# Attention weights stored as (query, four heads), with key tiles added in pairs for the denominator

## The reference

```python
q = (x @ Wq + bq).reshape(n, H, DK); k = ...; v = ...
logits = einsum('ehd,ehd->eh', q[rows] * scale, k[cols]) + att_bias
row_max = segment_max(logits, rows)
p = exp(logits - row_max[rows])
denom = segment_sum(p, rows)
att = p / denom[rows]
y = segment_sum(att[:, :, None] * v[cols], rows)
out = y.reshape(n, H * DK) @ Wo + bo
x = layernorm(x + out)
```

## Time and profile before

| | before |
|---|---|
| median of 3 runs (lowest to highest) | 1270.24 us (1258.51 to 1271.98) |
| profiled execution: span of the core | 1264.5 us |
| mean granted TensorE clock | 0.987 |
| PE busy | 1203.6 us (95%) |
| DVE busy | 864.5 us (68%) |
| ACT busy | 431.7 us (34%) |
| attention loop, first scores to last denominator product | about 982.6 to 1250.4 us of the span |

### The profile page before, as it was taken

The page is one execution under the profiler, slowest core; times in us unless marked ns, Lnnn a source line. Parts: engine busy times, 40 slices in busy tenths (PEclk is TensorE's granted clock), DMA queues, the critical chain, the costliest instruction groups (busy, mean ns, idle before and its releaser), DMA issues.

```text
span 1264.5 us, 22058 instructions
## 1 busy us (share of the span) xinstructions
PE 1203.6 (95%) x8483; PEld 547.2 (43%) x8484; DVE 864.5 (68%) x1180; ACT 431.7 (34%) x585; POOL 309.5 (24%) x220
## 2 busy tenths in 40 slices
PE   6989888999898999999999999999999999999997
PEld 2334333323443343344445454454332455555563
DVE  7577666434444555552478874658999799899897
ACT  1445556322232221213301003145551454444344
POOL 2001110000010243454555654555462000000000
PEclk9989999999998999999999999999999899999999
DMA  8568885798798788643122213113222666465552
GB/s 325 208 225 301 292 298 165 281 358 310 244 360 284 276 313 278 220 97 114 3 50 35 50 3 69 2 2 44 33 33 56 234 206 230 167 203 198 189 181 107
DMA packets 64414, 222.78 MB, mean 176 GB/s; under 512 B 31226, under 2 KB 36090, under 8 KB 48360
## 3 DMA queue, kind: packets, MB, share of 16 engines
q1 hardware_dynamic: 34794, 156.40, 35.6%
q0 software_dynamic: 25184, 53.10, 16.5%
q10 hardware_dynamic: 4350, 12.07, 2.8%
HBM read 198.94 MB, written 59.94 MB: 205 GB/s over the span
## 4 chain that ended last, share of the span: by engine, by line
PE 64%; DVE 11%; DMA 10%; issue 8%; SPq 5%; ACT 3%; ACTq 0%; DVEq 0%
PE PS L1812 24%; PE PS L1761 10%; PE PS L2057 4%; PE PS L1616 4%; PE PS L2044 4%; DMA R<-R 4%; DVE R L1147 4%; DVE R L1182 3%; PE PS L1634 3%; SPq L602 3%; PE PS L1686 2%; PE PS L1926 2%; SPq L600 2%; PE PS L2077 2%; PE PS L2106 2%
## 5 line engine op out<-in xcount | busy, mean ns | idle before, releaser
L787 POOL DMA_INDIRECT bias_d<-R x160 | 272.9, 1706 | 331.5 <-DMA bias_d<-R 220.2
L1812 PE MATMUL PS<-R 128*128 128x512 f16 x1300 | 298.4, 381 | 0.0
L1812 PEld LDWEIGHTS PS<-R 128*128 128x128 f16 x1300 | 120.5, 98 | 180.5 <-issue 49.8
L1572 ACT ACTIVATE R<-PS 128x1024 f32<-128x1024 f32 (+1 forms) x100 | 100.4, 1005 | 144.0 <-PE PS L2044 143.9
L1686 PE MATMUL PS<-R,XX 125*128 125x512 f16 (+2 forms) x612 | 131.0, 344 | 16.2 <-ACT R L1361 7.5
L1761 PE MATMUL PS<-W,XX 128*128 128x512 f16 x600 | 136.1, 386 | 4.7 <-DVE R L985 2.7
L1182 DVE SCALAR_TENSOR_TENSOR R<-R,W 128x1024 f32<-128x1024 f32 (+1 forms) x68 | 133.9, 1985 | 8.7 <-ACT R L1572 7.2
L1147 DVE CUSTOM_DVE_ANT_0 R<-PS,R 128x1250 f16<-128x1250 f32 x80 | 116.8, 1460 | 5.5 <-PE PS L1980 2.9
L901 DVE TENSOR_SCALAR R<-W,R 125x1250 f16<-125x1250 f16 x160 | 89.5, 606 | 42.4 <-PE PS L1686 27.6
L2044 PE MATMUL PS<-R 128*128 128x256 f16 (+3 forms) x800 | 107.4, 277 | 1.4 <-DVE R L1147 1.1
L2057 PE MATMUL PS<-R 128*32 128x256 f32 (+1 forms) x1600 | 105.7, 382 | 0.7 <-DVE R L1182 0.3
(11 more groups left out here) (226 smaller groups left out, 1395.6 us busy)
## 6 DMA issues: line engine op xcount, KB each, us to landing
bias_d<-bias_d POOLq DMA_DIRECT2D x39, 1280.0 KB, 8.5
R<-in_basis_s SPq DMA_DIRECT2D x32, 1024.0 KB, 6.6
W<-in_basis_s SPq DMA_DIRECT2D x28, 1024.0 KB, 6.3
W<-bias_d SPq DMA_DIRECT2D x27, 1024.0 KB, 4.9
R<-bias_d SPq DMA_DIRECT2D x13, 1024.0 KB, 5.0
R<-key_d SPq DMA_DIRECT2D x20, 500.0 KB, 3.8
R<-R SPq DMA_DIRECT2D x120, 80.0 KB, 5.9
W<-bias_d SPq DMA_DIRECT2D x7, 904.0 KB, 4.6
```

The source lines that it names most:

```text
L787: pool.indirect_dma_start(bias_d, bass.IndirectOffsetOnAxis(ap=idx[:, c:c + 1], axis=0), attr[:, c, :], None, bounds_check=DUMP + GC * P - ...
L1572: S.activation(ER[:, n % 4, :].rearrange("p (h r) -> p h r", h=4)[:, :, 0:w], PS[:, 2 * (n % 2):2 * (n % 2) + 2, :].rearrange("p a (e r) - ...
L1812: ins = T.matmul(mm_out(SUM_BANK(s, i), D), lhs, rhs, start=n == 0, stop=n == len(terms) - 1)
```

## The change

The weights now lie as (query, four heads) in `ER`. ACT writes each head's 256 values 16 bytes apart, DVE reads bias in runs of four neighbouring heads and weights in one run, and PE reads each head's columns in 16-byte steps. DVE adds the weights of two consecutive key tiles of the same head group into a buffer `SR` (two of them), and PE makes the denominator products from that sum once per two tiles. `ORDER` starts and ends with two key tiles in place of three for each group. The third bias buffer, the buffers `SR` and the f16 copy of Wo (`Wo16`) get other places in SBUF, so that SP's wait for the row maxima ahead of the third bias load is no longer needed and is left out.

```diff
--- before.py
+++ after.py
@@ -235,7 +235,8 @@
         bdf = tmp2(2 * EC).rearrange("p (g e) -> p g e", g=2)
         btf = tmp2(CH)
 
-        o = 2 * HEADS * NN // 2 + NN // 2 + RB
+        KEPT = 2 * HEADS * NN // 2 + NN // 2 + RB
+        o = KEPT
 
         def kept(n):
             nonlocal o
@@ -295,13 +296,20 @@
         o3 = NT * D + FT * RB
         y16 = XX[:, o3:o3 + FT * RB].bitcast(F16).rearrange("p (q f n) -> p q f n", q=2, f=FT)
         o3 += FT * RB
-        Wo16 = XX[:, o3:o3 + FT * D].bitcast(F16).rearrange("p (q f n) -> p q f n", q=2, f=FT)
-        assert o3 + FT * D <= NT * D + FT * NN
+        def quad_major(region):
+
+            return region.rearrange("p (r h) -> p r h", h=4)
+
         BW = 4 * RB
-        BR = [w_b[:, 0:2 * BW], w_b[:, 2 * BW:4 * BW], r1f[:, half:half + 2 * BW]]
-        ER = r1f[:, half + 2 * BW:half + 6 * BW].rearrange("p (s n) -> p s n", s=4)
-        assert 6 * BW <= half
+        BR = [w_b[:, 0:2 * BW], w_b[:, 2 * BW:4 * BW], XX[:, o3:o3 + 2 * BW]]
         NB = len(BR)
+        o3 += 2 * BW
+        SR = [quad_major(r) for r in (XX[:, o3:o3 + BW], r2[:, KEPT:KEPT + BW])]
+        assert o3 + BW <= NT * D + FT * NN and KEPT + BW <= NT * NN
+        Wo16 = r1f[:, half:half + FT * D].bitcast(F16).rearrange("p (q f n) -> p q f n", q=2, f=FT)
+        o4 = half + FT * D
+        ER = [quad_major(r1f[:, o4 + s * BW:o4 + (s + 1) * BW]) for s in range(4)]
+        assert FT * D + 4 * BW <= half
         Wo = W[:, 2, :, :]
 
         PS = ctx.enter_context(nc.psum_tensor("PS", [P, 8, 512], F32))
@@ -422,6 +430,7 @@
         st_done = sem("st_done")
         e_made = sem("e_made")
         p_made = sem("p_made")
+        sum_made = sem("sum_made")
         pv_done = sem("pv_done")
         den_read = sem("den_read")
         den_first_read = sem("den_first_read")
@@ -533,10 +542,17 @@
             return b16[32 * (n % 4):32 * (n % 4) + 2, n // 4, :], ones16[32 * (n % 4):32 * (n % 4) + 2, :]
 
 
-        ORDER = [(t, q) for q in range(QUADS) for t in range(NB)]
-        ORDER += [(t, q) for t in range(NB, NRB * NT - NB) for q in range(QUADS)]
-        ORDER += [(t, q) for q in range(QUADS) for t in range(NRB * NT - NB, NRB * NT)]
-        LATE = [n for n in range(STEPS - NB, STEPS)]
+        ORDER = [(t, q) for q in range(QUADS) for t in range(2)]
+        ORDER += [(t, q) for t in range(2, NRB * NT - 2) for q in range(QUADS)]
+        ORDER += [(t, q) for q in range(QUADS) for t in range(NRB * NT - 2, NRB * NT)]
+        PAIRS = [(ORDER.index((t - 1, q)), n) for n, (t, q) in enumerate(ORDER) if t % 2]
+        assert all(0 < b - a <= 2 for a, b in PAIRS)
+
+        def pair_of(n):
+            return [n in pair for pair in PAIRS].index(True)
+
+        def closes(n):
+            return ORDER[n][0] % 2 == 1
 
         def steps_done(rb, q):
 
@@ -704,7 +720,6 @@
             for t in range(2):
                 load_bias(t)
             max_row(1)
-            sp.wait_ge(s_used, NT * HEADS)
             load_bias(2)
             for t in range(NB, NRB * NT):
                 sp.wait_ge(p_made, max(n + 1 for n in range(STEPS) if ORDER[n][0] == t - NB))
@@ -1178,10 +1193,20 @@
                 dve.wait_ge(e_made, n + 1)
                 dve.wait_ge(bias_rd[t % NB], 16 * (t // NB + 1))
                 w = width(t // NT)
-                p = ER[:, n % 4, :].rearrange("p (h r) -> p h r", h=4)[:, :, 0:w]
-                V.scalar_tensor_tensor(p, p, BIG,
-                                       BR[t % NB].rearrange("p (r h) -> p h r", h=HEADS)[:, 4 * q:4 * q + 4, 0:w],
-                                       ALU.min, ALU.mult).then_inc(p_made, 1)
+                p = ER[n % 4][:, 0:w, :]
+                b = BR[t % NB].rearrange("p (r h) -> p r h", h=HEADS)[:, 0:w, 4 * q:4 * q + 4]
+                V.scalar_tensor_tensor(p, p, BIG, b, ALU.min, ALU.mult).then_inc(p_made, 1)
+
+            def weights_added(n):
+
+                k = pair_of(n)
+                first, second = PAIRS[k]
+                w = width(ORDER[n][0] // NT)
+                dve.wait_ge(p_made, second + 1)
+                if k >= 2:
+                    dve.wait_ge(pv_done, PAIRS[k - 2][1] + 1)
+                V.tensor_tensor(SR[k % 2][:, 0:w, :], ER[first % 4][:, 0:w, :], ER[second % 4][:, 0:w, :],
+                                ALU.add).then_inc(sum_made, 1)
 
             def denominators(rb):
                 dve.wait_ge(pv_done, QUADS * NT * (rb + 1))
@@ -1250,9 +1275,11 @@
             for n in range(STEPS):
                 rb, m = divmod(n, QUADS * NT)
                 weigh(n)
-                if rb and m == 0:
+                if closes(n):
+                    weights_added(n)
+                if rb and m == 1:
                     denominators(rb - 1)
-                if rb and m in (1, 3, 6, 8):
+                if rb and m in (2, 3, 6, 8):
                     inverted(rb - 1, m // 6, m in (3, 8))
                 if rb and m in (4, 9):
                     divided(rb - 1, m // 9)
@@ -1568,8 +1595,9 @@
                 act.wait_ge(st_done, n + 1)
                 if n >= 4:
                     act.wait_ge(pv_done, n - 3)
+                    act.wait_ge(sum_made, pair_of(n - 4) + 1)
                 w = width(rb)
-                S.activation(ER[:, n % 4, :].rearrange("p (h r) -> p h r", h=4)[:, :, 0:w],
+                S.activation(ER[n % 4][:, 0:w, :].rearrange("p r h -> p h r"),
                              PS[:, 2 * (n % 2):2 * (n % 2) + 2, :].rearrange("p a (e r) -> p (a e) r", e=2)[:, :, 0:w],
                              ACT.Exp, scale=DK ** -0.5).then_inc(e_made, 1)
                 if rb and m in (0, 1):
@@ -2032,7 +2060,7 @@
                 rb, j = divmod(t, NT)
                 if n >= 2:
                     pe.wait_ge(e_made, n - 1)
-                if n in (0, NB):
+                if n in (0, 2):
                     pe.wait_ge(mrow_in[q], 16)
                 if n < 2:
                     pe.wait_ge(s_used, NT * HEADS - 1 + n)
@@ -2055,17 +2083,14 @@
                 for e in range(2):
                     for i in range(4):
                         ins = T.matmul(PS[32 * i:32 * i + 32, 4 + q, e * RB:e * RB + w],
-                                 VA[:, j, 4 * q + i, 32 * e:32 * e + 32], ER[:, n % 4, i * RB:i * RB + w],
+                                 VA[:, j, 4 * q + i, 32 * e:32 * e + 32], ER[n % 4][:, 0:w, i],
                                  start=j == 0 and e == 0, stop=j == NT - 1, skip_group_check=True)
-                if n in LATE[0:-1]:
-                    ins.then_inc(pv_done, 1)
-                    return
-                if j == 0 and rb:
-                    pe.wait_ge(den_read, rb)
-                if n == LATE[-1]:
-                    pe.wait_ge(den_first_read, 1)
-                for step_ in LATE if n == LATE[-1] else [n]:
-                    ins = denominator(step_)
+                if closes(n):
+                    if j == 1 and rb:
+                        pe.wait_ge(den_read, rb)
+                    if n == STEPS - 1:
+                        pe.wait_ge(den_first_read, 1)
+                    ins = denominator(n)
                 ins.then_inc(pv_done, 1)
 
             def denominator(n):
@@ -2073,10 +2098,12 @@
                 t, q = ORDER[n]
                 rb, j = divmod(t, NT)
                 w = width(rb)
+                k = pair_of(n)
+                pe.wait_ge(sum_made, k + 1)
                 for i in range(4):
                     ins = T.matmul(PS[32 * i:32 * i + 32, 6, q * RB:q * RB + w], ones[:, 0:32],
-                                   ER[:, n % 4, i * RB:i * RB + w],
-                                   start=j == 0 and q == 0, stop=j == NT - 1, skip_group_check=True)
+                                   SR[k % 2][:, 0:w, i],
+                                   start=j == 1 and q == 0, stop=j == NT - 1, skip_group_check=True)
                 return ins
 
             def projected_bias(i):
```

## The result

The changed kernel takes **1361.6 us** (median of 4 runs, 1358.8 to 1366.4) against 1269.7 for the kernel before, measured beside it (4 runs, 1258.5 to 1272.0): ratio **1.075, 95% interval 1.071 to 1.079**. The prediction was 1255; the measured time lies 4 us above its range and inside the 1332 to 1370 of its first rival. The profiled execution has a span of 1364.5 us and took 1366.4.

What follows compares the result with a forecast made beforehand. PE's own work was taken to fill the block, DVE 10% below. Denominators -21.7, lumps +4, ACT's writes +1, start +1.5 and the rest +0.5 gave -14.7 from 1270.2, put at 1255 us; range 1246 to 1358.

Steps and rivals of the forecast that it cites:

- first rival: PE pays for 16-byte steps as DVE does for its step, factor 1.75 to 2.1: 1332 to 1370 us, chance 0.28.
- PE's reads in 16-byte steps: no price: PE's streamed weight columns: stay at 0.868 ns despite the step; upper end 1.825 ns; called the sum's weakest step.
- The two bounds, 0.868 and 1.825: PE's ns per fp32 weight column: contiguous pace as lower end, DVE's time per stepped element as upper end.
- Denominators, -21.7: PE's denominator products: fifty of a hundred steps lose their eight matmuls, 0.444 us each (0.39 in the last block).
- Weighing 1.29, additions 1.21: DVE's us per weighing and per pair addition of 1024 elements; DVE's block about 46.5, under PE's 50.2.
- The lumps, +4: DVE's uneven work in a block's first ten steps stalls PE at the sum: +1 us a block, +4 (0 to 7).
- ACT's writes, 1.6 us and +1: ACT's exp with 16-byte writes: 1.6 us, between 1.03 and 2.05; later weights shorten DVE's lead, +1 (0 to 2).
- the 50.2 of PE's work: PE's forecast work in a row block of the loop: 54.6 less 4.4 us for the denominators saved.
- Start, +1.5: Loop start: third scores wait for the second group's maxima; third products at 998 against 995.83, +1.5 us (0 to 4).
- The range: Whole kernel's time, eight in ten: 1246 to 1358 us, leaving out the worst of the first rival.
- The signs that the prediction named for the first rival: Changed profile: sixteen matmuls of products with V take 1.56 to 1.87 us, not 0.89; DVE idle a quarter of the loop.

Runs made afterwards that it cites:

- with contiguous reads: Changed kernel, but PE reads each 256 columns of the weight and sum buffers as neighbouring elements (heads get each other's weights): 1258.45 us, ratio 0.993.
- the faster weighing alone: Kernel before with only the weights' layout changed to (query, four heads), PE reading runs, no sums: 1264.01 us, ratio 0.999.
- two heads: Changed kernel with weights as two pieces of (query, two heads), 8-byte steps for PE and ACT, weighing in two instructions: 1255.78 us, ratio 0.993.
- the first probe: Kernel before plus unused matmuls after PE's work, streamed operand in steps of 4 to 64 bytes (fp32), 2 to 32 (f16): 1.76 ns a column, fp32 alone, 16 bytes.

## Why the prediction was wrong

- *PE's reads in 16-byte steps: no price.* This step failed, and it alone put the time outside the range. The measured factor is 2.03 (0.868 to 1.76 ns), so the first rival came true near its upper end, 2.1: with 2.03 its own sum gives 89.6 + 0.7 + 1.5 = +91.8 us, and +91.9 was measured. The two bounds, 0.868 and 1.825, did hold the value; the choice between them was wrong. The prediction argued that an f16 column every 0.43 ns shows a stream that "can take a new place" that often. But eight neighbouring f16 columns lie in one 16-byte line, so that row shows a new line only every 3.4 ns, and the fp32 row one every 3.5. No row of PE that the prediction read came near a line for each column; the f16 row was evidence on columns, not on lines. The row that did bear on it was DVE's with one element a line, 1.825 ns, and the prediction set it aside as another engine's. Measured at a line for each element: DVE 1.83 ns, PE 1.76 ns, ACT's copy 2.00 us for 1024.
- The Trainium skill's note ("SBUF — State Buffer", Door 1, on cachelines), which the prediction cited against its own choice, was right on the line's 16 bytes, as the pair across a line's end shows. Its two hits are nearly enough for fp32 (7.36 us against 6.91 without a step), but not for f16: two of every eight cost 3.61 against 1.76, while four of eight were nearly free (1.83).
- *Denominators, -21.7.* Right at the old price: with contiguous reads an undisturbed step takes PE 2.43 us with denominators and 2.00 without, so a block loses the ten times 0.44. At the new price half the denominators at twice the time save next to nothing against the kernel before.
- *Weighing 1.29, additions 1.21.* Measured 1.22 and 1.23; DVE's block 45.82 for a forecast 46.5. The 5.4 us of the earlier trace rows are waits of PE's weight loads, most of them while PE was still at work: with the faster weighing alone the loop shrank by 1.2 us.
- *The lumps, +4, and ACT's writes, 1.6 us and +1.* With contiguous reads the block is 1.9 us over the 50.2 of PE's work, not 1. Over the loop the late starts of PE's groups (each against its usual distance from the one before) add up to 9.0 us in place of 4 and 1, and to 1.8 with two heads; with the start's +2.0 (below) the sum would be -10, and that kernel gained 9.2 (by its ratio 4 to 13). The exp took 2.00, the upper of its two ends, so the lead that was to cover part of the lumps was shorter. In the changed kernel both are hidden behind PE.
- *Start, +1.5.* With contiguous reads the third products begin 15.2 us after the loop's first scores (13.2 before), +2.0. The wait for the second group's maxima (4.2 us there, 4.6 in the changed kernel) is the one that was foreseen.
- *The range.* It ended at 1358, where the first rival's factor is 2, though the rival's own upper end was 1370. With 0.28 on it, and its rows at 1.75 to 2.1, its upper part should not have been cut.

The signs that the prediction named for the first rival are all there: products with V in 1.79 us (1.56 to 1.87 forecast), and DVE idle for over a third of the block (27.5 of 73.3; a quarter of the loop forecast).

## What to carry to other kernels

Before laying data out for one engine, count for every other engine that reads or writes it how many 16-byte lines of a partition it touches for an element, and price those at about 1.76 ns each (PE's time here; DVE and ACT came near it) against the engine's own pace. Runs of two fp32 within a line were nearly free for PE, ACT and DVE here, so a layout with two heads beside each other gave DVE its gain without taking it from PE. And a row at full speed bounds only what it exercises: neighbouring columns say nothing of how fast lines can change.

## What the runs showed of the hardware

The price is a time and didn't follow PE's granted clock. At the loop's start in the changed kernel, after PE's wait of 4.57 us for the maxima, the granted clock was 0.50 (the 1.2 GHz level) from 997.88 to 1001.62 us. The scores ran at their slow 1.87 us, yet the products after them took what they take later at the full clock: 1.95 us to the next scores, and 1.94 then.

```profile
997.88 1.87 PE L2072 MATMUL PS<-R 128*128 128x256 f16 x8 [4.57 <-DMA R<-max_d]
999.67 2.02 PE L2085 MATMUL PS<-R 128*32 128x256 f32 x16
...
999.67:1001.62 1.95, 1.95 (x17) 0.55 (x17) 0.00 (x0) 1.84 (x1) 0.00 (x0) 0.50 0.44 185
```

In the changed kernel with contiguous reads, the same products took 1.94 us at that clock, and 1.07 two steps on at the full one:

```profile
991.37 1.94 PE L2087 MATMUL PS<-R 128*32 128x256 f32 x16
...
997.24 1.07 PE L2087 MATMUL PS<-R 128*32 128x256 f32 x16
```

So at the slow clock fp32's own pace (1.94 us for 1024 columns of a pass) happens to lie near the price of a line, and f16, whose pace is faster, shows the price more plainly. In the first probe the clock fell during the f16 row at 16 bytes, after PE had just taken f16 columns in 8-byte steps, and the f16 row at 32 bytes ran at 0.50 throughout:

```profile
1345.40:1352.87 7.47, 7.47 (x19) 1.89 (x17) 0.00 (x0) 0.00 (x0) 0.00 (x0) 0.50 0.00 0
```

That is 1.82 ns a column for 4096 of them; fp32 columns with the same step took 1.80 at the full clock. Without a step the clock sets the time, with one the lines do. Beside that, ACT writes and DVE reads at nearly PE's price for a line, although the three engines have different paces; and an f16 stream falls to half speed already when it takes two of every eight elements (3.61 us against 1.76), where fp32 with two elements a line loses nearly nothing (1.82 against 1.75).
